# Row sums straight behind the second half of P V, with their rest on VectorE

## The reference

```
q = x @ Wq ; k = ctx @ Wk ; v = ctx @ Wv          # 16 heads of 64
logits = (q k^T) * 64**-0.5 + col_bias            # bias on 2 + 2 key columns
probs = softmax(logits) ; out = (probs @ v) @ Wo + bo + x
```

## Time and profile before

| quantity | value |
|---|---|
| median of three runs | 3416.62 us (3416.29 to 3416.98) |
| profiled execution, its own time | 3416.71 us |
| its span, first to last instruction | 3414.9 us |
| TensorE busy | 3294.7 us, 96% |
| VectorE, GpSimd busy | 2531.0 us, 2512.9 us, 74% each |
| ScalarE busy | 2184.4 us, 64% |

### The profile page before, as it was taken

One profiled execution on the slowest core, in us unless ns is written; L12 is line 12 of the kernel. 1 busy time (PEld: TensorE's weight loads), 2 busy tenths in 40 slices (PEclk: granted clock), 3 DMA queues, 4 the chain that ended last, 5 costly groups with the idle time before them and its releaser, 6 DMA issues.

```text
span 3414.9 us, 72963 instructions
## 1 busy us (share of the span) xinstructions
PE 3294.7 (96%) x28066; PEld 1559.2 (46%) x28066; DVE 2531.0 (74%) x4668; ACT 2184.4 (64%) x2690; POOL 2512.9 (74%) x1218
## 2 busy tenths in 40 slices
PE   6999999999998898889999999999999999999998
PEld 3445544445443322234454455444444554444553
DVE  6677777777767788856787777777667777777776
ACT  5466666666546777764666666666546666666665
POOL 6888888888752000128888888888888888888887
PEclk9999999999999999999999999999999999999999
DMA  4000000000000000000000000000000000000000
GB/s 156 3 11 11 2 11 11 11 1 9 6 10 13 10 9 17 17 1 11 11 9 3 11 11 2 11 11 11 1 11 11 1 11 11 11 1 11 3 2 26
DMA packets 50195, 42.29 MB, mean 12 GB/s; under 512 B 4928, under 2 KB 42176, under 8 KB 49856
## 3 DMA queue, kind: packets, MB, share of 16 engines
q1 hardware_dynamic: 49136, 37.08, 3.6%
q10 hardware_dynamic: 720, 0.53, 0.1%
HBM read 32.36 MB, written 2.10 MB: 10 GB/s over the span
## 4 chain that ended last, share of the span: by engine, by line
PE 90%; ACT 3%; DVE 2%; issue 2%; POOL 2%; DMA 0%; SPq 0%; ACTq 0%; DVEq 0%; POOLq 0%
PE ps_j L917 40%; PE ps_st L1068 14%; PE ps_j L1108 11%; PE ps_j L1121 6%; PE ps_sm L1000 6%; PE ps_st L1053 3%; PE ps_j L1095 3%; ACT pt L1596 2%; PE ps_sm L1082 2%; PE ps_j L1154 1%; PE ps_st L1000 1%; POOL acc L754 1%; PE ps_j L1009 1%; PE ps_j L1170 1%; PE ps_j L1145 0%
## 5 line engine op out<-in xcount | busy, mean ns | idle before, releaser
L754 POOL TENSOR_TENSOR acc<-acc,pt 128x1024 f32<-128x1024 f32 x570 | 1366.3, 2397 | 261.1 <-ACT pt L1596 207.5
L1596 ACT ACTIVATE pt<-ps_st 128x1024 f32<-128x1024 f32 x768 | 742.7, 1019 | 301.0 <-PE ps_st L1068 289.1
L2063 DVE CUSTOM_DVE_ANT_0 ps_sm<-ps_sm,bias_m,nmx 128x512 f32<-128x512 f32 x666 | 479.8, 756 | 184.7 <-PE ps_j L1000 148.9
L917 PE MATMUL ps_j<-w_h,ctx_h 128*128 128x128 f16 x3072 | 531.5, 220 | 2.3 <-ACT rinv L1612 1.1
L917 PE MATMUL ps_j<-w_h,ctx_l 128*128 128x128 f16 x3072 | 530.5, 219 | 0.0
L917 PE MATMUL ps_j<-w_l,ctx_h 128*128 128x128 f16 x3072 | 530.5, 219 | 0.0
L2063 DVE CUSTOM_DVE_ANT_0 ps_sm<-ps_sm,bias_m 128x512 f32<-128x512 f32 x486 | 334.6, 707 | 160.5 <-PE ps_j L1000 147.8
L1108 PE MATMUL ps_j<-pt,v 128*64 128x512 f32 x1792 | 409.2, 598 | 0.0
L783 POOL TENSOR_TENSOR o_un<-o_un,rinv 128x512 f32<-128x512 f32 x111 | 142.2, 1281 | 320.0 <-ACT rinv L1608 294.5
L2100 DVE RECIPROCAL rinv<-rinv 128x256 f32<-128x256 f32 x190 | 331.1, 1745 | 14.1 <-ACT rinv L1612 4.4
L2053 DVE TENSOR_REDUCE nmg<-ps_st 128x2 f32<-128x1024 f32 x248 | 295.9, 1218 | 43.7 <-PE ps_st L1000 42.5
(11 more groups left out here) (200 smaller groups left out, 6592.8 us busy)
## 6 DMA issues: line engine op xcount, KB each, us to landing
w_raw<-wk SPq DMA_DIRECT2D x25, 256.0 KB, 2.8
pt<-ctx_t SPq DMA_DIRECT2D x6, 1024.0 KB, 7.3
w_raw<-wv SPq DMA_DIRECT2D x24, 256.0 KB, 3.6
wo_raw<-wo SPq DMA_DIRECT2D x28, 128.0 KB, 2.0
w_raw<-wq SPq DMA_DIRECT2D x24, 128.0 KB, 3.0
k_h<-k_l SPq DMA_DIRECT2D x72, 32.0 KB, 2.0
x<-x_t SPq DMA_DIRECT2D x4, 512.0 KB, 8.5
acc<-ctx_t SPq DMA_DIRECT2D x2, 1024.0 KB, 8.4
```

The costliest lines, as they stand in the source:

```text
L754: G.tensor_tensor(total, first, pt[:, n % RING, :], ALU.add).then_inc(s_acc, 1)
L917: done = MM(dst, l, r, start=first and i == 0, stop=last and i == n - 1)
L1596: A(pt[:, n % RING, :], src.rearrange("p h q -> p (h q)"), ACT.Exp).then_inc(s_exp, 1)
L2063: last = V.tensor_tensor_reduce(out=src, in0=src, in1=bias_m[:, t, half * HALF:(half + 1) * HALF], scale=-1.0, scalar=nmx[:, 0, t, h:h + 1 ...
```

## The change

For a new predicate `early_sums(p)`, true where the slot `p + 1` is turned and does not split x, four things change. TensorE makes the sums straight behind the second half of P V, ahead of `score_block(1)`. In the order of the banks the sums move to the other shared bank, and the opening unit of block 1 takes the bank that `pvb` has just used. VectorE, no longer GpSimd, makes `acc_l`, ahead of `second_half`; GpSimd only waits for it before it goes on. ScalarE runs `sums_out` ahead of the exponentials of block 1, no longer behind them. Slots that split x, the slots of layer 1 and slots 29 to 31 keep their order.

```diff
+def early_sums(p):
+
+    return not grouped(p) and turned(p + 1) and not splits_x(p + 1)
...
-            if past:
-                then("sum" if grouped(s - 1) else "pvb", s - 1, a)
-            opening(1, 1 - a)
-            if past:
-                then("rb" if grouped(s - 1) else "sum", s - 1, a)
+            if past and early_sums(s - 1):
+                then("pvb", s - 1, a)
+                then("sum", s - 1, 1 - a)
+                opening(1, a)
+            else:
+                if past:
+                    then("sum" if grouped(s - 1) else "pvb", s - 1, a)
+                opening(1, 1 - a)
+                if past:
+                    then("rb" if grouped(s - 1) else "sum", s - 1, a)
```

GpSimd:

```diff
-                if past and split_sums(s - 1):
+                if past and early_sums(s - 1):
+                    pool.wait_ge(s_acc_l, splits(s - 1) + 1)
+                elif past and split_sums(s - 1):
                     sums_lo(s - 1)
```

TensorE, in `turned_slot`:

```diff
                 if past and not grouped(s - 1):
                     attend(s - 1, 1)
-                elif past:
+                if past and (grouped(s - 1) or early_sums(s - 1)):
                     sums(s - 1)
                 score_block(1)
-                if past and not grouped(s - 1):
+                if past and grouped(s - 1):
+                    rows_of_reciprocals(s - 1)
+                elif past and not early_sums(s - 1):
                     sums(s - 1)
-                elif past:
-                    rows_of_reciprocals(s - 1)
```

ScalarE, in `turned_slot`:

```diff
+                if past and early_sums(s - 1):
+                    sums_out(s - 1)
                 exponentials_of(1)
-                if past:
+                if past and not early_sums(s - 1):
                     sums_out(s - 1)
```

VectorE, the new function:

```diff
+            def sums_lo(p):
+                dve.wait_ge(s_acc_h, splits(p) + 1)
+                V.tensor_tensor(acc_l, acc[:, p % 2, :], acc_h, ALU.subtract).then_inc(s_acc_l, 1)
```

and in its `turned_slot`:

```diff
+                if past and early_sums(s - 1):
+                    sums_lo(s - 1)
                 if past and not grouped(s - 1):
                     second_half(s - 1)
```

## The result

The changed kernel takes 3425.59 us, the median of eight runs (3424.09 to 3428.22), against 3416.45 us (3414.81 to 3419.25, eight runs) of the kernel before. The ratio is 1.0027, with a 95% interval of 1.0017 to 1.0036: slower, by 9 us. The forecast was 3426 us.

A forecast was written before the change was run, and what follows sets the result against it. TensorE, busy 96% of the span, was taken to bound the kernel. 84 slots x (0.07 + 0.01) = 6.7 us plus 2.4 for token rows gave 9.1 us over the kernel before: 3426 us, range 3421 to 3431.

The forecast's parts named there:

- Which engine decides: Whole kernel: TensorE, busy 29.21 of a turned slot's 29.30 us; a 0.1 us delay in a slot delays the kernel.
- What is saved: Sums moved behind P V's second half: one tile-change drain less on TensorE, 0.12 to 0.17 us a slot.
- The operand: `acc_l` on VectorE ahead of the sums: takes 1.22 us, done at 61.72, sums start at 61.87.
- The wait for the bank: Block 1's opening unit waits for `second_half` to read `pvb`'s bank, starting at 62.88, not 62.73: slot 0.07 us longer.
- What is late next: VectorE behind the closing unit: first reciprocal 0.37 us later, `k1` ahead of the second key projection 0.01 us late.
- Token rows: Six slots with 1.28 us `token_rows` steps ahead of `sums_lo`: opening unit 0.4 us later each, 2.4 us in all.
- Sum: 84 slots x (0.07 + 0.01) = 6.7 us, plus 2.4 us for token rows: 9.1 us slower.
- the free bank (faster): Rival at the opening unit: bank free in time, drain saving of 0.12 to 0.17 whole, 3405 to 3409 us; chance 0.13.
- Slower by VectorE's queue: Rival: first reciprocal starts only behind the last accumulator read, `k1` waits 0.15 us, 3437 us; chance 0.12.
- Slower by `acc_l`: Rival: VectorE's subtraction takes 2.00 us, opening unit 0.63 later, 3475 us; tells from 1.37 us; chance 0.05.
- The wait and the drain: Rival at the opening unit: bank wait and saved drain cancel within 0.2%, 3414 to 3423 us; chance 0.25.

The follow-up runs named there:

- the run with its own place and turned banks: Changed kernel, sums in half of `ps_sm`, block 1's opening unit in its old bank, then the two shared banks change roles: 3411.49 us, ratio 0.9986.
- GpSimd's rest: Changed kernel, but GpSimd makes the rest of the row sums (`acc_l`) as before the change: 3487.84 us, ratio 1.0207.

## Why the prediction was right

- **Which engine decides.** TensorE, slot by slot. The work that changed engine is worth nothing by itself: 1.0003 (0.9994 to 1.0011).
- **What is saved.** I gave 0.12 to 0.17 us a slot; the run with its own place and turned banks shows 0.12.
- **The operand.** Reckoned to take 1.22 us and to end at T + 3.38; it took 1.23 and ended at 3.40. I had the sums at T + 3.53 and they came at 3.49, where they come without the wait too. The 0.15 us of the earlier trace rows doesn't hold behind this instruction; it is 0.05 where TensorE does wait for it (last section).
- **The wait for the bank.** Forecast for the opening unit T + 4.54, measured 4.54. The wait itself is 0.20 us, not 0.15, as the sums came earlier; that changes nothing in the slot, since the end of `second_half` decides. The place is shown from both sides: with a bank of its own the unit comes at 4.34 or 4.35, and in the kernel before with that bank alone it comes at 4.54.
- **What is late next.** First reciprocal 0.37 later, as forecast, and no wait ahead of the second key projection: a slot of 29.37 us, where I gave 29.37 to 29.38.
- **Token rows.** Forecast 0.4 over the other slots for six slots, measured 0.27, 0.28 and 0.40. The cause is the forecast one, a late operand. Slot 10 (T is 351.69), TensorE and VectorE:

```profile
351.69 3.65 PE L1120 MATMUL ps_j<-pt,v 128*64 128x512 f32 x16
355.62 0.62 PE L1166 MATMUL ps_j<-sq,ones_h_sb 128*64 128x512 f16 x4 [0.28 <-DVE sq L2103]
...
353.15 1.28 DVE L2022 SCALAR_TENSOR_TENSOR y_rms<-iota_sb,tok_f,y_rms 128x1024 f16<-128x1024 f16 x1
354.35 1.22 DVE L2103 TENSOR_TENSOR sq<-acc,sq 128x1024 f16<-128x1024 f32 x1
```

  The rest starts 0.08 before the record ahead of it ends, and the sums start 0.05 behind the rest, where I had put 0.15. So they come at T + 3.93 and not at 4.08, and the opening unit at 4.81 and not at 4.94. In slot 12 the rest starts 0.04 behind the token step's end, and the opening unit comes at 4.94.
- **Sum.** Forecast 9.1 us; the 84 slots show 8.6, the medians 9.1, the two profiled executions 10.1. The agreement to a tenth is luck: the ordinary slots took 0.07 and not 0.08, and the token rows 1.9 us and not 2.4, while slots 28 and 110 (0.23 and 0.43) were summed as ordinary ones. What holds those two wasn't tried.

Of the rivals, the free bank (faster) has the right price, 0.12 a slot, and the wrong condition: the bank isn't free in time. Slower by VectorE's queue didn't come: the first reciprocal starts at 2072.63, beside the last read of the accumulator, and the second key projection doesn't wait. Slower by `acc_l` didn't come either: 1.23 us, under the 1.37 from which it would tell. The wait and the drain don't cancel: 0.07 us a slot is left, and the interval, 1.0017 to 1.0036, leaves out 1.

## What to carry to other kernels

Where products share PSUM banks, moving one of them changes who follows whom in a bank, and the wait that comes with it can cost more than the move saves. So reckon the time at which each bank is read out beside the order of the products. When one such wait is taken away, look at the next user of the bank: here the gain came only when the wait had been taken out at both places.

A large VectorE instruction on SBUF beside GpSimd has no fixed price. It depends on which of the two comes first: here 0.06 us too late cost VectorE 1.7 us, and 0.08 us ahead cost it nothing and GpSimd 1.1.

## What the runs showed of the hardware that I had not expected

- The shutting out works both ways, and in the cases shown all but some 0.15 us of the later instruction came behind the earlier one: VectorE's 1.23 us became 2.56, its 1.9 became 3.63, and GpSimd's 1.16 became 2.21.
- The hand-over to TensorE is not one number. Behind `second_half` it was 0.15 us in each kernel whose opening unit waited for it. Behind the rest of the sums it was 0.05 us, where TensorE truly waited for it: in slot 10 of the changed kernel (above), behind GpSimd's rest, and without GpSimd's wait (2128.29 + 2.56 = 2130.85 to the sums at 2130.90):

```profile
2130.90 0.62 PE L1164 MATMUL ps_j<-sq,ones_h_sb 128*64 128x512 f16 x4 [1.12 <-DVE sq L2101]
```
